# CTR kernel with three attention layers: two units' values in one transfer, and transposes ahead of the scores in even steps

## What is computed

```python
embed_x = emb_table[X + offsets[None, :]]            # 2048 x 39 x 64
for i in range(3):
    q, k, v = x @ Wq, x @ Wk, x @ Wv                 # 2 heads of 32
    attn = softmax(einsum('bihd,bjhd->bhij', q, k))
    x = relu(einsum('bhij,bjhd->bihd', attn, v) + x @ Wr)
att = relu(x.reshape(B, 39 * 64) @ Wlin)
h = relu(embed_x.reshape(B, 39 * 64) @ W1 + b1); h = relu(h @ W2 + b2)
out = sigmoid(att + relu(h @ W3 + b3))
```

## Time and profile before

| | us |
|---|---|
| median of 3 runs | 2241.02 |
| lowest, highest | 2228.72, 2245.64 |
| the profiled execution | 2240.81 |
| its span (first to last instruction) | 2239.0 |
| granted TensorE clock over the span | 0.994 of full speed |

### The profile page before, as it was taken

One profiled execution on the slowest core, in us unless ns is written; L12 is line 12 of the kernel. 1 busy time (PEld: TensorE's weight loads), 2 busy tenths in 40 slices (PEclk: granted clock), 3 DMA queues, 4 the chain that ended last, 5 costly groups with the idle time before them and its releaser, 6 DMA issues.

```text
span 2239.0 us, 134899 instructions
## 1 busy us (share of the span) xinstructions
PE 2079.7 (93%) x57568; PEld 1686.5 (75%) x57568; DVE 1774.3 (79%) x5105; ACT 1211.1 (54%) x3187; POOL 1245.5 (56%) x1838
## 2 busy tenths in 40 slices
PE   1099999999999999999999999999999999999998
PEld 0077877878777787877778787777878778788787
DVE  3077878878888788888888787888888888788887
ACT  0055655555555555655555555555656555565554
POOL 7627476473756647376574747647374674731403
PEclk9999999999999999999999999999999999999998
DMA  5112122221222222122222222222122222212221
GB/s 144 32 44 69 48 64 54 54 65 47 67 50 58 55 51 70 48 66 53 56 61 50 67 50 62 55 54 63 47 69 50 62 58 53 64 47 51 49 50 33
DMA packets 169081, 128.06 MB, mean 57 GB/s; under 512 B 46040, under 2 KB 155880, under 8 KB 168488
## 3 DMA queue, kind: packets, MB, share of 16 engines
q1 hardware_dynamic: 148520, 98.95, 17.5%
q0 software_dynamic: 19968, 20.49, 4.7%
HBM read 27.24 MB, written 0.01 MB: 12 GB/s over the span
## 4 chain that ended last, share of the span: by engine, by line
PE 83%; DVE 9%; issue 4%; POOL 3%; another core or an unknown queue 0%; DMA 0%; ACT 0%; ACTq 0%
PE SV L431 22%; PE Mb L388 14%; PE Ob L455 14%; PE X L440 12%; PE X L411 11%; POOL emb L284 3%; PE Ob L417 2%; PE Ob L418 2%; PE Ob L419 2%; PE Mb L366 2%; DVE pn L646 2%; DVE den L624 2%; DVE sd L640 1%; PE Mb L401 1%; DVE x_lo L609 1%
## 5 line engine op out<-in xcount | busy, mean ns | idle before, releaser
L284 POOL DMA_INDIRECT emb<-L_rec_emb_table,idx_t x624 | 629.2, 1008 | 207.5 <-issue 202.9
L630 DVE TENSOR_REDUCE mx<-SV 103x8 f32<-103x312 f32 x768 | 369.1, 481 | 410.4 <-PE SV L431 346.7
L431 PE MATMUL SV<-yv,xs 64*39 64x71 f32 x12288 | 576.6, 227 | 0.3 <-issue 0.2
L539 ACT COPY yv<-X 128x312 f32<-128x312 f32 x768 | 286.3, 426 | 527.7 <-PE X L411 513.3
L431 PE MATMUL SV<-yv,xw 64*39 64x71 f32 x12288 | 566.4, 227 | 0.4 <-issue 0.2
L431 PEld LDWEIGHTS SV<-yv,xs 64*39 64x39 f32 x12288 | 445.2, 112 | 154.1 <-ACT yv L539 97.4
L553 ACT ACTIVATE pe_sb<-sd 103x312 f32<-103x312 f32 x768 | 358.9, 467 | 175.6 <-DVE sd L640 170.6
L269 POOL COPY xs<-embT 64x256 f32<-64x256 f32 x300 | 196.6, 655 | 437.2 <-DVE x_lo L609 415.7
L440 PE MATMUL X<-ident,pn 103*103 103x103 f32 x3072 | 438.6, 265 | 0.6 <-issue 0.6
L431 PEld LDWEIGHTS SV<-yv,xw 64*39 64x39 f32 x12288 | 434.5, 112 | 1.0 <-issue 0.5
L568 ACT COPY pt<-X 103x312 f32<-103x312 f32 x768 | 320.7, 418 | 191.4 <-PE X L440 184.9
(11 more groups left out here) (73 smaller groups left out, 2554.5 us busy)
## 6 DMA issues: line engine op xcount, KB each, us to landing
xw<-xs SPq DMA_DIRECT2D x768, 78.0 KB
v_x<-v_sb SPq DMA_DIRECT2D x1536, 19.5 KB
emb<-L_rec_emb_table,idx_t POOLq DMA_INDIRECT x624, 2.5
w<-L_rec_W SPq DMA_DIRECT2D x1, 4864.0 KB
w<-L_rec_W SPq DMA_DIRECT2D x1, 512.0 KB
idx_in<-r_X SPq DMA_DIRECT2D x1, 312.0 KB, 3.8
b_b<-L_rec_b SPq DMA_DIRECT2D x1, 256.0 KB
w<-L_rec_W SPq DMA_DIRECT2D x1, 128.0 KB
```

The lines of the kernel that those rows point to most:

```text
L284: nc.gpsimd.indirect_dma_start(out=emb[:, f * D:(f + 1) * D], out_offset=None, in_=table, in_offset=bass.IndirectOffsetOnAxis(ap=idx_t[:, ...
L431: last = nc.tensor.matmul(SV[u % 2][64 * b:64 * b + F, at:at + YR], x_pair(u, e, p, h), yv[64 * r:64 * r + D, l, e, slot, p, :], start=Tru ...
L630: nc.vector.tensor_reduce(mx[:, v % 2].rearrange("q r g -> q (r g)"), sv_scores(v), AX.X, ALU.max).then_inc(mx_ready, 1)
```

## The change

Two parts. The values of units 2d and 2d+1 are moved by one DMA for each direction, when both have been copied to `v_sb`; SyncE's loop runs over pairs, with three semaphores `v_moved`, one for two slots. And in even steps TensorE does the transposes, with their wait for `y_ready`, ahead of the scores.

```diff
-        v_moved = [sem(f"v_moved{k}") for k in range(VS)]
+        v_moved = [sem(f"v_moved{k}") for k in range(VS // 2)]
...
             exchange(0)
-            for s in range(STEPS):
-                if s % 2 == 0 and s // 2 + 1 < TOTAL // 2:
-                    exchange(s // 2 + 1)
-                u = s - SV_AT
-                if 0 <= u < TOTAL:
-                    sp.wait_ge(v_ready, u + 1)
-                    for b in range(2):
-                        lo, hi = 64 * b, 64 * (1 - b)
-                        sp.dma_start(v_x[hi:hi + F, u % VS, :, :],
-                                     v_sb[lo:lo + F, u % VS, 1 - b, :, :]).then_inc(v_moved[u % VS], 16)
+            for d in range(TOTAL // 2):
+                if d + 1 < TOTAL // 2:
+                    exchange(d + 1)
+                slot = 2 * d % VS
+                sp.wait_ge(v_ready, 2 * d + 2)
+                for b in range(2):
+                    lo, hi = 64 * b, 64 * (1 - b)
+                    sp.dma_start(v_x[hi:hi + F, slot:slot + 2, :, :],
+                                 v_sb[lo:lo + F, slot:slot + 2, 1 - b, :, :]).then_inc(v_moved[slot // 2], 16)
...
-                pe.wait_ge(v_moved[u % VS], 32 * (u // VS + 1))
+                pe.wait_ge(v_moved[u % VS // 2], 32 * (u // VS + 1))
...
                     if s < TOTAL:
                         dense(t, ts)
-                    if 0 <= s - SV_AT < TOTAL:
-                        scores(s - SV_AT)
                     if 0 <= tu < TOTAL:
                         pe.wait_ge(y_ready, min(s + 1, TOTAL))
                         transposes(tu)
+                    if 0 <= s - SV_AT < TOTAL:
+                        scores(s - SV_AT)
```

## The result

The median is 2256.6 us (11 runs, 2242.0 to 2260.4) against 2239.5 us (11 runs of the kernel before beside them, 2228.7 to 2249.6): a ratio of 1.0063, 95% interval 1.0037 to 1.0089. That is within 1%. The profiled execution took 2250.5 us, its span 2248.7: 9.7 us more than the span before, where 69 were forecast.

The account below looks back on a forecast made before the run. TensorE was taken as the pace mostly, beside a VectorE latency loop from even scores to x_lo with 0.25 us margin; 27.7 + 12.3 + 29.4 = 69.4 us of waits on 2240.8 gave 2310 us, 3.1% slower, range 2258 to 2345.

Parts of the forecast that it names:

- (a): SyncE's value transfers, two a pair instead of four: nobody waits for them, so zero gain and cost on the path.
- Rival 2: Pairs under gathers: halving SyncE's transfers removes late signals, 43 us back at most, 2220 us in all; chance 0.07.
- (b): Exchanges in SyncE's queue go out one pair later, with 2.3 to 3.9 us left to land: cost taken as zero.
- rival 3: Exchanges land late, so scores wait for xw: 60 to 126 us in gather pairs, 2370 us; chance 0.05.
- (c): TensorE's even steps, transposes ahead of scores: scores and x_lo come 0.36 us later, costing 69.4 us together.
- Rival 1: Even scores start only 0.16 us later, a shift shorter than x_lo's margin: 2258 us, no change; chance 0.13.
- rival 4: Even steps' transposes keep their 0.54 us behind dense too: 130 us more, 2371 us; chance 0.05.

Follow-up runs that it names:

- e3: Kernel before, its four value transfers a pair issued together after the second copy, behind the next pair's exchange, one pair later than before: 2395.8 us, 1.073.
- e2: Kernel before with only TensorE's order in even steps changed, transposes ahead of scores, four value transfers a pair kept: 2300.1 us, ratio 1.029.
- e5: Changed kernel with VectorE's x_lo moved ahead of den (the row sums), 0.39 us earlier: 2232.9 us, ratio 0.998.
- e9a: e4 plus two spare transfers a pair that nobody needs, one number in each of 39 partitions: 2238.1 us, ratio 0.999.
- e9b: e4 plus two spare transfers a pair that nobody needs, one number in a single partition: 2219.3 us, ratio 0.990.
- e4: e1 with each exchange issued a pair earlier, where it stood in the kernel before: 2193.8 us, ratio 0.980.
- e1: Changed kernel with TensorE's order of before, so only the value transfers are paired and exchanges come later: 2198.8 us, ratio 0.984.

## Why the prediction was wrong

**The step that failed is (a), "Gain and cost on the path: zero".** Transfers alone give -38.6 us by the spans, -1.6% by the runs. The argument asked who waits for SyncE's transfers and found no one; that holds after the change too. But four of them a pair beside the gathers go with 0.41 us more a pair on average, two with 0.10: part is TensorE's late signals, which in a list of waits stand under TensorE and VectorE, and part is stalls inside attended, which the list of waits does not show as a wait for anybody. The earlier trace rows had shown the 1.80 us, and the text called its reason unknown; a term with an unknown cause then went into the sum as a constant.

**Rival 2 had the place, the size and half of the mechanism** (43 us at most, in 126 pairs; measured 40.8 in 127 pairs of places 12 to 19). It had the late signals go with the transfers, and they do, but it knew nothing of the stretched attendeds, so that the size fits so well is in part luck. It was weighed at 7% as another case instead of the forecast. The two don't exclude each other: the forecast's order cost and rival 2's gain add. Its argument against was the stretch without gathers, which goes at 5.2 with as many transfers; that shows only that transfers alone do no harm, not that transfers beside gathers do none. By its own price, 2241 - 43 + 22, it came to 2220, since it also took the gather pairs' share of the shift away. The order still costs 17.6 us there alone, and with the two parts together these places give 18.6 instead of 40.8.

**(b), the exchanges, is right.** No wait for xw in the change. In the rows of SyncE's queue an exchange is out at 1115.10 (1113.93 + 1.17), and its scores start at 1118.83 in TensorE's timeline: 3.7 us to land, forecast 2.3 to 3.9. e3 shows how near rival 3 was: with 3.22 us of issue instead of 1.83 the kernel is 7% slower, a part of it at a lower clock. The landing of up to 2.7 us there is longer than the 2.3 that the worse case had left.

**(c), the order, is right in mechanism and 10 us or more high in size.** Measured alone +59.7 by the spans, forecast 69.4; about 5 us of the measured is e2's lower clock, so the forecast is some 15 us high (an estimate). Undisturbed pair 5.34 (forecast 5.33), even transposes 0.36 (0.36), scores 2.04 behind F on average (2.04), residual's first product 0.34 in the chain of e5 (0.35), 308 waits (some 300), matmul share 92% (about 90%), y_ready 9.4 us (taken as nothing, at most 29). By classes: 127 undisturbed pairs +15.9 in e2 (112 x 0.11 = 12.3 forecast); places 0, 1, 12 to 21 and 23 together +47.7 (27.7 + 29.4 = 57.1); places 2, 3 and 22 -4.5 (0).

**Rival 1 is out**, since the scores moved by the whole 0.36, and so is rival 4: the transposes take 0.36 behind an even dense too. The sentence that would have them at 0.54 (the Trainium skill, page "TensorE: Matmul & The Clock Gate", Part 3, "The mechanism") is again not borne out by the trace. The same section also lets a load go ahead when it targets the background weight buffer, and the trace does not contradict that.

**What the two parts do together** looks less than their sum: +9.7 against -38.6 + 59.7 = +21. The table by place has the difference at 20, 21, 23 and at 22, where the half clock falls. In place 22 a pair takes 5.99 on average before, 6.23 with the transfers alone and 5.71 in the change, but the median is 5.61 in each. With the clock's share out, it is +14 against -44 + 54 = +10, so most of the gap was the clock.

**What stays open.** Shown is that fewer of SyncE's issues near the gathers take away most of the late signals and of the stretched attendeds, that bytes aren't what counts, and that it happens nowhere else. Not shown is the path by which it happens, whether through the issue, the completion or something that GpSimd's gathers share with them, and how much of it is the number of issues and how much the phase of the pairs against the gathers. Gathers from another queue, or none, and transfers issued by another engine weren't tried.

## To carry to other kernels

When a signal comes late in one stretch for no reason that the trace names, measure first whether the engine's own work stretches there too. Then price what the change does to everything else that runs in that stretch, even if nobody waits for it; and put a gain that can stand beside the forecast into the sum or the range, not among the exclusive rivals. A change of two parts is forecast for each part alone first: here +2.9% and -1.6% read as 0.6%. Before two traces are compared place by place, the stretches at a lower clock come off. And fewer, larger transfers from a queue shared with other work can pay although the queue is idle part of the time.

## What the runs showed of the hardware

- A spare transfer of one number in each of 39 partitions holds SyncE's queue for 0.79 us (median of 768 in e9a), one of one number in one partition for 0.62 (e9b), one of 39 rows of 256 numbers for 0.9. Two of the first kind a pair take the ratio from 0.980 (e4) to 0.999 (e9a), some 41 us.
- With six of SyncE's issues a pair beside gathers TensorE's signal to VectorE comes 0.15 to 0.37 us late on average (0.96 in e9b to 1.18 before, against 0.81 away from gathers), and 0.15 to 0.30 us a pair is lost inside the 64 small matmuls of the two attendeds. With four and before's order it is 0.05 and 0.03 at most (e1, e4). Without gathers six cost nothing.
- VectorE doing x_lo ahead of den, the same instructions in another order, raised that delay in each of the three bases: 1.18 to 1.54, 0.94 to 1.19, 0.85 to 1.26 us.
- What is late is the signal and not VectorE: the maxima start 0.02 us after the semaphore's update in undisturbed pairs and under gathers alike, wherever the trace has the update (before).
- A pair of 5.61 us with 3.4 us of half clock in it takes 7.0 to 7.3.
